# Order of instructions in the first three gaps of a four-layer graph attention kernel

## The reference

```python
def layer0(x, adj, W_heads, a1, a2, W_out, b_out):      # 8 heads
    Wh = einsum('nf,hfd->hnd', x, W_heads)
    e = leaky_relu(s1[:, :, None] + s2[:, None, :], 0.2)  # s1 = Wh.a1, s2 = Wh.a2
    att = softmax(where(adj > 0, e, -9e15), axis=-1)
    hp = elu(att @ Wh)
    return concat_heads(hp) @ W_out + b_out
h = relu(layernorm(x)); x = x + layer0(h, adj, ...)
h = relu(layernorm(x)); x = x + gelu(attention(h))        # layer 1, one head
h = relu(layernorm(x)); x = x + elu(attention(h))         # layer 2
h = relu(layernorm(x)); x = x + elu(attention(h))         # layer 3
```

## Time and profile before

| | us |
|---|---|
| median of 3 runs | 776.5 (775.86 to 779.19) |
| the profiled execution, device time | 776.41 |
| its span, first to last instruction | 774.7 |
| TensorE busy | 750.0 (97%) |
| VectorE busy | 626.4 (81%) |
| ScalarE busy | 328.8 (42%) |
| mean granted TensorE clock | 0.988 of full speed |

### The profile page before, as it was taken

How to read it: one execution, slowest core, us unless ns; L and a number is a source line. 1 busy time by engine, 2 the same in 40 slices (tenths; PEclk the granted TensorE clock), 3 DMA queues, 4 the chain that set the end, 5 groups by cost and what they waited for, 6 DMA issues and landing times.

```text
span 774.7 us, 15961 instructions
## 1 busy us (share of the span) xinstructions
PE 750.0 (97%) x6451; PEld 731.0 (94%) x6451; DVE 626.4 (81%) x1042; ACT 328.8 (42%) x888; POOL 16.1 (2%) x36
## 2 busy tenths in 40 slices
PE   8899899999999999999999999999889989998997
PEld 7699799999999999999999999999789969996997
DVE  4896788797877978879788796888588949997986
ACT  5875562343543246134354334623441244535420
POOL 3000000000000000000000000000000000000000
PEclk9999999999999999999999999999999989999999
DMA  9794000000000000000000000000000000000001
GB/s 298 269 364 159 28 2 28 27 0 27 2 25 27 0 27 0 27 27 0 27 17 10 27 0 27 0 0 2 0 2 1 1 1 1 2 1 1 1 19 38
DMA packets 13874, 29.39 MB, mean 38 GB/s; under 512 B 1296, under 2 KB 7568, under 8 KB 13840
## 3 DMA queue, kind: packets, MB, share of 16 engines
q1 hardware_dynamic: 11152, 20.00, 7.6%
q0 software_dynamic: 2688, 8.92, 3.4%
HBM read 27.80 MB, written 1.11 MB: 37 GB/s over the span
## 4 chain that ended last, share of the span: by engine, by line
PE 85%; ACT 5%; DMA 4%; DVE 4%; issue 1%; SPq 0%; DVEq 0%; ACTq 0%
PE acc L409 49%; PE acc L432 25%; DMA stage<-in_adj_t_dram 4%; PE side L509 3%; PE side L365 3%; PE acc L483 2%; ACT adjT L623 1%; DVE probs L1070 1%; ACT hpT L716 1%; DMA W0t<-in_W_t_dram 1%; PE side L471 1%; ACT hT L834 0%; PE side L457 0%; PE side L491 0%; ACT xn L825 0%
## 5 line engine op out<-in xcount | busy, mean ns | idle before, releaser
L409 PE MATMUL acc<-V,probs 128*128 128x129 f32 x3840 | 438.1, 276 | 1.9 <-DVE probs L1064 1.9
L409 PEld LDWEIGHTS acc<-V,probs 128*128 128x128 f32 x3840 | 434.0, 192 | 4.9 <-ACT V L657 2.7
L1070 DVE SCALAR_TENSOR_TENSOR probs<-rho,t_now,adjT 128x1024 f32<-128x1024 f32 x224 | 272.9, 1277 | 11.4 <-PE acc L409 9.1
L1166 DVE SCALAR_TENSOR_TENSOR probs<-rho,t_now,adjT 128x768 f32<-128x768 f32 (+3 forms) x179 | 146.7, 880 | 9.6 <-PE acc L432 6.6
L716 ACT ACTIVATE hpT<-rows 32x256 f32<-32x256 f32 x224 | 92.8, 414 | 71.1 <-DVE rows L1107 68.6
L432 PEld LDWEIGHTS acc<-stage,probs 128*128 128x128 f32 x1024 | 115.0, 192 | 4.0 <-ACT stage L865 3.7
L432 PE MATMUL acc<-stage,probs 128*128 128x129 f32 x1024 | 116.1, 275 | 2.1 <-DVE probs L1166 2.1
L432 PE MATMUL acc<-V,probs 128*128 128x129 f32 x768 | 89.4, 275 | 0.0
L432 PEld LDWEIGHTS acc<-V,probs 128*128 128x128 f32 x768 | 87.4, 192 | 1.0 <-ACT V L865 0.9
L1115 DVE TENSOR_TENSOR X<-X,side 128x512 f32<-128x512 f32 x28 | 19.3, 688 | 65.0 <-PE side L509 65.0
L701 ACT ACTIVATE fill<-mean_now,empty 128x128 f32<-128x128 f32 x112 | 34.2, 397 | 87.9 <-DVE den L1083 87.9
(11 more groups left out here) (190 smaller groups left out, 416.6 us busy)
## 6 DMA issues: line engine op xcount, KB each, us to landing
stage<-in_adj_t_dram SPq DMA_DIRECT2D x32, 512.0 KB, 7.0
rho<-rho_dram POOLq DMA_DIRECT2D x15, 512.0 KB, 3.9
X<-in_x_dram SPq DMA_DIRECT2D x2, 512.0 KB, 4.4
W0t<-in_W_t_dram SPq DMA_DIRECT2D x1, 512.0 KB, 5.1
W<-in_L_gnn_W_heads_dram SPq DMA_DIRECT2D x1, 512.0 KB, 6.4
Wout<-in_L_gnn_W_out_dram POOLq DMA_DIRECT2D x1, 512.0 KB, 10.4
out_dram<-X SPq DMA_DIRECT2D x1, 512.0 KB, 3.7
out_dram<-X SPq DMA_DIRECT2D x1, 384.0 KB, 3.0
```

The source lines that it names most:

```text
L409: last = nc.tensor.matmul(group(c, k), probs[:, j % RING, k * P:(k + 1) * P], V[:, j, :], start=(j == 0 and k % PER_BANK == 0), stop=(j == ...
L1070: nc.vector.scalar_tensor_tensor(probs[:, j % RING, :], rho[:, c * CH:(c + 1) * CH], t_now[:, j:j + 1], adjT[:, j, c * CH:(c + 1) * CH], A ...
L1166: return nc.vector.scalar_tensor_tensor(slot_of(n, p, j)[:, first:end], rho[:, at + first:at + end], t_now[:, j:j + 1], adjT[:, j, at + fi ...
```

## The change

Four things are reordered, and nothing else is computed.

1. **Layer 0, ScalarE.** The fill tiles of unit 0 go between the casts: after block 27 and ahead of blocks 28 to 31. For every later unit the fill follows at the end of the work before it, which leaves ScalarE's sequence of instructions in the loop the same, with the loop's edge moved to behind the fill. The last head's pass stands outside the loop, written out. The fill of the last first half now counts on `fill_ready`.
2. **Hole 1.** The transposes and projections of the six tiles (part 1 of layer 0) stand some tiles sooner in TensorE's program. The four `keep_warm` products are gone. The normalised six tiles are transposed ahead of the two ELU tiles. On VectorE the statistics and scaling of the six tiles stand ahead of the denominators of the two; ScalarE's order follows.
3. **Hole 2, ScalarE.** GELU of the six tiles stands ahead of `keep_wh`; both score copies and then the table load stand after the ReLU of the six tiles. On TensorE the second score product stands behind the transposes of the six tiles.
4. **Hole 2, VectorE.** The two tiles' inverse root in layer 2 is taken by three Newton steps on VectorE instead of ScalarE's Ln and Exp.

```diff
@@ scalar, layer 0
-            def finish(u, c):
+            def fill_for(u, c):
                 act.wait_ge(rden_ready, u + 1)
                 fill_rows(c)
-                nonlinear(u, ACT.Exp)
-                move_blocks(u)
+
+            def next_head(h):
+                nonlinear(2 * h, ACT.Exp)
+                move_blocks(2 * h)
+                nc.scalar.activation(v_now[:, :], v_all[:, bass.ds(h + 1, 1), :].rearrange("p a t -> p (a t)"),
+                                     ACT.Copy).then_inc(tv_ready, 1)
+                act.wait_ge(tv_ready, h + 3)
+                scale_v(h + 1)
+                fill_for(2 * h + 1, 1)
+                nonlinear(2 * h + 1, ACT.Exp)
+                move_blocks(2 * h + 1)
+                take_mean(mean_w[:, bass.ds((h + 1) * D, D)], h + 2)
...
-            cast(22, 2 * NT)
-            with act.Fori(0, H - 1) as h:
-                finish(2 * h, 0)
...
+            cast(22, NT + 12)
+            fill_for(0, 0)
+            cast(NT + 12, 2 * NT)
+            with act.Fori(0, H - 2) as h:
+                next_head(h)
+                fill_for(2 * h + 2, 0)
+            next_head(H - 2)
@@ tensor, hole 1 and hole 2
                 late_s1(n, 0, wh_kept, n)
-                late_s1(n, 1, wh_kept, n)
+                if n != 2:
+                    late_s1(n, 1, wh_kept, n)
                 if n == 1:
-                    pe.wait_ge(late_rows, 4)
-                    keep_warm(WARM, warm_bank)
+                    transpose_normed(1, 1, 0, x_written, chunk_no(1, 1, 0))
+                    transpose_normed(1, 1, 1, x_written, chunk_no(1, 1, 1))
                     transpose_rows(2, 0, wh_kept, 1)
                     project_rows(2, 0)
-                    transpose_normed(1, 1, 0, x_written, chunk_no(1, 1, 0))
-                    transpose_normed(1, 1, 1, x_written, chunk_no(1, 1, 1))
...
+                if n == 2:
+                    late_s1(n, 1, wh_kept, n)
...
-            late_unit(0, 2, {(9, 1): lambda: transpose_rows(1, 0, hT_ready, 1),
-                             (10, 1): lambda: transpose_rows(1, 1, hT_ready, 2),
-                             (11, 1): lambda: project_rows(1, 0),
-                             (13, 0): lambda: project_rows(1, 1)})
+            late_unit(0, 2, {(7, 0): lambda: transpose_rows(1, 0, hT_ready, 1),
+                             (8, 1): lambda: transpose_rows(1, 1, hT_ready, 2),
+                             (10, 0): lambda: project_rows(1, 0),
+                             (11, 0): lambda: project_rows(1, 1)})
@@ scalar, hole 2
                     nonlinear_late(2, 1)
+                    keep_wh(2)
                     late_normed(2, 1)
                     nonlinear_late(2, 2)
-                    nc.scalar.preload_act_table_set(LOG_EXP)
-                    late_inverse_root(2, 2)
                     late_relu(2, 1, 0)
                     late_relu(2, 1, 1)
                     keep_s1(2, 0)
+                    keep_s1(2, 1)
+                    nc.scalar.preload_act_table_set(LOG_EXP)
                     late_relu(2, 2, 0)
-                    keep_s1(2, 1)
@@ vector
-                if n == 2 and p < 2:
+                if n == 2:
...
+            late_statistics(1, 1)
+            late_scale(1, 1)
             late_denominators(1, 2)
             late_divide(1, 2, 0)
-            late_moments(1, 1)
+            late_norm(1, 1)
             late_elu_rows(2, 0)
-            late_variance(1, 1)
-            late_scale(1, 1)
-            late_norm(1, 1)
             add_to_x(1, 2, 0)
```

More of the change, by code:

```diff
@@ L253, in root_no @@
         def root_no(n, p):
-            return {(1, 0): 1, (1, 1): 2, (1, 2): 3, (2, 2): 4, (3, 0): 5, (3, 1): 6, (3, 2): 7}[n, p]
+            return p + 1 if n == 1 else p + 4
         def chunk_bank(p, i):
@@ L933, in _ @@
                     late_inverse_root(1, 2)
+                    keep_s1(1, 1)
                     late_relu(1, 2, 0)
@@ L1216, in late_divide @@
                 dve.wait_ge(late_rden, stage_no(n, p))
-                dve.wait_ge(late_fill, c + 1 if n == 1 else n)
+                if n == 1 and c == 0:
+                    dve.wait_ge(fill_ready, 4 * H - 2)
+                else:
+                    dve.wait_ge(late_fill, n if n == 1 else n - 1)
                 if n == 1 and p:
```

21 lines of the change are left out of this document (8 added, 13 removed).

## The result

The changed kernel takes 767.42 us (median of 4 runs, 767.40 to 767.65) against 776.35 us before (775.86 to 779.19): ratio 0.9879, 95% interval 0.9862 to 0.9895. The medians are 8.9 us apart. The profiled execution took 767.65 us with a span of 766.0, where before had 776.41 and 774.7.

The account below looks back on a forecast made before the run. TensorE, busy for 97% of the span, was taken to bound the kernel, so only its waits and slow stretches counted. The sum was 776.41 - 5.15 - 1.3 - 2.75 = 767.21, so 767.2 us, range 765.8 to 771.3.

Parts of the forecast that it names:

- First gap: TensorE's wait before unit 0's projection in layer 0: earlier fill was to save 5.15 us, bounds 3.0 to 5.4.
- the term for the wait: First gap: fill ahead of the last four casts lets ELU start 3.5 us sooner.
- The clock's term: First gap: with the clock staying up, the projection's 16 records take 1.95 instead of 3.60 us, another 1.65.
- Hole 1: Hole 1: the two tiles' transposes come at 561.2 instead of 562.49, saving 1.3 us; bounds 0.1 to about 1.8.
- 0.1 if the 5.59 stay whole: Hole 1's lower bound: 0.1 us if the two tiles still need 5.59 us from denominators free to addition.
- rival (c): Holes: nothing gained, since the new order only exchanges who waits; 771.3 us, chance 0.05.
- Hole 2: Hole 2: 2.75 us saved, 1.7 from the earlier start and 1.07 from the tail's clock; bounds 1.7 and 3.0.
- GELU can start 1.6 us sooner and all follows: Hole 2: the six tiles' GELU, freed from three row copies, starts 1.6 us sooner, and their later steps follow.
- the ReLU of the six stood behind load, Ln and Exp, and it now follows the GELU: Hole 2: ReLU at about 629.5, so TensorE's products come at 630.7 and end near 632.0 at full clock.
- (a): Clock falls late in hole 1 or 2: 768.3 to 769.9 for one, 771 or more for both; chance 0.25.
- (b): First gap's wait shrinks, but TensorE restarts at the low clock or casts drag: 768.9 to 769.3; chance 0.08.
- (d): Slower: ScalarE stalls at the loop's new edge, once per head; 776.4 + 3.9 needs 13.1 us; chance 0.02.

Follow-up runs that it names:

- e11: The changed kernel itself run once more, on the same chip as two combined kernels; 768.12 us (765.89 to 768.70).
- e10: e9 plus four unread products ahead of the last transposes in holes 1 and 2; 765.62 us (765.15 to 766.51).
- e6: Changed kernel with hole 2's table load and the two tiles' Ln and Exp back ahead of the six tiles' ReLU, no Newton steps; 767.18 us.
- e2: Kernel before with the change's hole 1 edits alone; 775.03 us (770.72 to 777.35), 0.9977 of before.
- e8: Changed kernel with hole 1 ordered for the two tiles on VectorE, ScalarE and TensorE; 766.25 us (765.84 to 766.79).
- e5: Changed kernel with hole 2's row copies ahead of the six tiles' GELU again; 770.14 us (768.60 to 770.68).
- e4: Changed kernel with the four unread products back in hole 1, right behind the score products; 767.76 us (767.39 to 768.40).
- e7: Changed kernel with unit 0's exponentials between its last casts, behind block 28 and ahead of blocks 29 to 31; 768.10 us (766.88 to 768.28).
- e12: e9 plus four unread products ahead of the last transposes in hole 1 only; 764.94 us (764.64 to 765.63).
- e9: Changed kernel with the edits of e8, e7 and e6 together; 765.23 us (764.64 to 766.13).

## Why the prediction was right

767.2 us was forecast, 767.42 measured; but the terms were off in opposite ways, and one reason was partly wrong. Against the profiled execution (767.65 us) the first gap gave 0.86 us less than forecast and the holes 0.43 more. That the sum comes out this near is partly luck, and so is the execution: it is one of two among the eleven profiles with hole 1's edit in which the clock's fall cost nothing there.

**First gap: 5.15 forecast, 4.29 measured.** The mechanism is as described: fill early, casts behind it, chain forward, clock up. Oversized was the term for the wait, 3.5: in the changed kernel's profile block 27 was cast at 63.30 instead of 62.36, because it landed later, and everything behind stood 0.7 to 0.9 us later than worked out (ELU at 71.56 instead of 70.8). I had taken the landing times of one execution as fixed. They move: over the fourteen profiles block 27 is cast between 61.08 (e11) and 64.23 us (e10), and the old gap's price moves with them. The clock's term, 1.65, was 1.54. In the mean of the profiles the block behind the projection starts at 86.8 us with the old order and at 83.2 with the new, which is 3.7 us, so the term was oversized by more than this pair shows. The 0.3 us of wait that my sum left was 0.79 here and up to 1.61 (e6), and the clock stayed up behind each.

**Hole 1: 1.3 forecast, 1.52 measured.** Each step came as worked out: Ln 0.5 us into the hole, the two tiles' denominators delayed to the end of scaling, their addition 6.1 us in (6.4 forecast), the six tiles' products hidden though slow. e2 has the same gain alone, up to the start of hole 2. The bound "0.1 if the 5.59 stay whole" and rival (c) had their truth: the two tiles do pay for the six, and e8 removes that payment, so that the last transposes come 1.4 us sooner still.

**Hole 2: 2.75 forecast, 2.96 measured.** The sum was right, and the step "GELU can start 1.6 us sooner and all follows" was the right one (e5: 2.1 us lost without it, 0.4 of it by the clock). The step "the ReLU of the six stood behind load, Ln and Exp, and it now follows the GELU" is true of the old order, where TensorE's products of the six waited for that ReLU and the two tiles' transposes, normalised at 633.73, came behind them at 635.09:

```profile
633.14 2.15 PE L483 MATMUL acc<-WL,hT 128*128 128x129 f32 x12 [2.37 <-ACT hT L834]
```

But moving the load away was not needed. By e6, with the load left on ScalarE ahead of that ReLU, the last transposes come sooner still. Once GELU is early, the load ends exactly when the two tiles' statistics do, and Ln, Exp and one step beat eleven Newton steps by more than the ReLU loses. I had worked out the Newton steps' price (1.1 us) and not set it against the order without them. The clock stayed up, as in six of the nine later profiles that have GELU ahead of the copies; in the other three (e4, e7, e8) its tail cost 0.15 to 0.4 us.

**Rivals.** (a), the clock falling late, is real, was thought too rare and was overpriced. I gave it 0.25; in hole 1 it came in nine of the eleven profiles with that edit, e11's of the same kernel among them. I priced it at 1.07 to 2.7 us per hole. By the distances from the last transposes to the next hole it cost 0.2 to 0.5 us in hole 1 and 1.5 once (e11), and 0.2 to 0.3 in hole 2. The old tail of 6.38 us, from which I took the price, is what it costs when the clock is already low at the transposes; usually it falls behind them. My sum for both holes, "771 or more", does not follow from the prices either: twice 1.07 gives 769.3. The late fall in hole 1 and the scatter ahead of the first gap both go into the changed kernel's 765.9 to 768.7 us from run to run. The rule of the Trainium skill on transposes and the clock (TensorE: Matmul & The Clock Gate, PE-mode transpose) is not decided here: with the unread products (e4) and without them (e6, e7, e11) the clock fell in hole 1 at about the same place. (b) did not come: the distance behind the projection is 1.78 to 1.89 us in every profile with the new order. (c) did not come as a whole. (d), a stall at the loop's new edge, is absent: the 463.59 us behind the first projection are the same before and after. On the table load, the traces show that the next instruction may start 0.02 us after its 1.28 us when it is ready, in before and e6 with Ln, and nothing like the 1.38 us of draining that the Trainium skill adds (ScalarE: Activation LUTs, What ACT_TABLE_LOAD costs).

What stays open is how far the clock's fall can be steered: e10 and e12 suggest a little, but two profiles are too few against something that shifts by itself. Open too is why the clock falls in the first blocks in eleven of the fourteen profiles and not in three.

## What to carry to other kernels

Where the last few tiles end a stretch, order every engine for them first, and put the bulk's work into their waits; the change had it half the other way and left 1.4 us. Before a table load is traded for arithmetic on another engine, look whether it can end inside a wait that is there anyway: here it could, and the trade cost 0.3 us. When a kernel's runs scatter, compare lengths of stretches inside the profiles: in e2 they showed 1.5 us where a dozen runs said 0.3 to 3.3, and they showed that the scatter up to hole 1 is made ahead of the block behind the first projection, by the old gap and by the clock in the first blocks.

## What the runs showed of the hardware

- The same code restarts at either clock after a wait of 2.4 to 3.8 us: after 3.77 us at the low one (16 records in 3.60 us), after 2.76, 2.40 and 1.61 us at the full one (2.05 us).
- In the holes the clock's fall changes place from one execution to the next, with the work unchanged: twelve records of projection took 2.87 us in the changed kernel and 1.61 in e11, the last score products 1.88 and 3.62 us.
- The clock also falls at TensorE's first blocks of layer 0, from about 24 us on, and for how long differs between executions: the same 32 records took 4.02 us in e5, e6 and e9 with the granted clock at 1.00, 5.29 to 5.45 in nine profiles and 6.72 and 6.75 in e7 and e2 with windows at 0.50. With it the denominators of the first unit come between 59.98 and 62.19 us.
- A late start of the first block is sometimes made good in part: with a tail of 5.82 us in e2 the layer behind it took 59.84 instead of 60.13 us. With nearly the same tails in e4 and e9 it took 60.13, so this cannot be counted on; no run here separates the cause.
